# A fused conditioning block and graph attention on one core: modulation weights in two transfers, a new order and engine assignment, and V of two chunks spread by SBUF transfers

## What is computed

```python
# layer 0: block with adaptive modulation, 16 heads of 8
cmod = silu(c) @ w_ada + b_ada          # 6 x 128: shift, scale, gate, twice
x_mod = ln(x) * (1 + scale) + shift
k, q, v = split(x_mod @ w_qkv, 3)
y = softmax((q / 8) @ k.T) @ v
x = x + gate * (y @ w_proj + b_proj)
x = x + gate2 * (gelu(modulate(ln(x)) @ w_mlp1 + b_mlp1) @ w_mlp2 + b_mlp2)
# layer 1: graph attention, two directions, keys and values are the first 20 tokens
self = concat(x, where(rowsum(x) == 0, 0, c)) @ W_self.T + b_self
for d in range(2):
    aff = where(adj_d.sum(-1) > 0, q_d @ k_d.T / sqrt(8), NEG) + adj_d @ w_bias + b_bias
    out += per_head(softmax(aff) @ self[:, :20], Wout[d]) + bout[d]
return x + relu(self + out)
```

## Time and profile before

| | us |
|---|---|
| median of 3 runs | 98.25 |
| the three runs | 97.46, 98.25, 98.9 |
| the profiled execution | 97.81 |
| its span, first to last instruction | 96.1 |
| PE busy | 84.2 (88%) |
| DVE busy | 64.9 (68%) |
| POOL busy | 59.9 (62%) |
| ACT busy | 46.6 (49%) |

### The profile page before, as it was taken

The page is one execution under the profiler, slowest core; times in us unless marked ns, Lnnn a source line. Parts: engine busy times, 40 slices in busy tenths (PEclk is TensorE's granted clock), DMA queues, the critical chain, the costliest instruction groups (busy, mean ns, idle before and its releaser), DMA issues.

```text
span 96.1 us, 4165 instructions
## 1 busy us (share of the span) xinstructions
PE 84.2 (88%) x1806; PEld 67.8 (71%) x1806; DVE 64.9 (68%) x165; ACT 46.6 (49%) x103; POOL 59.9 (62%) x83
## 2 busy tenths in 40 slices
PE   0999974899999999799999999999999999959600
PEld 0999952577758867658887888787887878738600
DVE  2407989844995989847487500796869989757471
ACT  4600239569755339491804695353426545146300
POOL 6862996509980303547336199758099899876660
PEclk9999999669999999999999999999999999999975
DMA  1999995000000000000000011002000020322021
GB/s 39 268 303 391 335 283 147 0 0 3 7 7 0 7 0 10 0 0 7 3 0 0 10 24 43 7 0 59 20 12 0 21 50 14 84 59 61 3 61 55
DMA packets 3634, 5.75 MB, mean 60 GB/s; under 512 B 704, under 2 KB 2752, under 8 KB 3488
## 3 DMA queue, kind: packets, MB, share of 16 engines
q1 hardware_dynamic: 3352, 5.05, 18.4%
q10 hardware_dynamic: 264, 0.44, 1.3%
HBM read 4.22 MB, written 0.52 MB: 49 GB/s over the span
## 4 chain that ended last, share of the span: by engine, by line
PE 65%; DMA 10%; DVE 7%; POOL 5%; ACT 3%; SPq 3%; issue 3%; POOLq 1%
PE ps_s L965 12%; DMA home_a<-in_adj 10%; PE ps_b L887 7%; PE ps_b L893 7%; PE ps_b L867 6%; PE ps_b L820 5%; PE ps_b L983 4%; PE ps_b L912 4%; PE ps_b L837 3%; PE ps_b L1013 3%; PE ps_b L991 3%; PE ps_b L914 2%; PE ps_b L920 2%; ACT home_b L1115 2%; POOL home_a L625 2%
## 5 line engine op out<-in xcount | busy, mean ns | idle before, releaser
L619 POOL TENSOR_TENSOR E<-E,neg_max 128x640 f32<-128x640 f32 x8 | 10.2, 1276 | 5.7 <-DVE neg_max L1337 5.7
L1047 ACT ACTIVATE Kb<-ps_b,head_mask 128x256 f32<-128x256 f32 (+1 forms) x20 | 7.3, 434 | 7.5 <-PE ps_b L867 7.5
L1125 ACT ACTIVATE PT<-ps_b 120x384 f32<-120x384 f32 x16 | 7.4, 490 | 6.9 <-PE ps_b L983 6.8
L789 POOL TENSOR_TENSOR rstd<-var_eps,minus_half 128x2 f32<-128x2 f32 (+1 forms) x9 | 5.9, 667 | 6.7 <-DVE var_eps L1159 6.6
L723 POOL TENSOR_TENSOR Kb<-k_raw,head_mask 128x640 f32<-128x640 f32 x8 | 9.9, 1260 | 0.2 <-ACT k_raw L1078 0.2
L611 POOL TENSOR_TENSOR xT<-gated,xT 128x256 f32<-128x256 f32 x8 | 5.8, 727 | 6.3 <-DVE gated L1200 6.3
L723 POOL TENSOR_TENSOR Vz<-v_raw,quad_mask 128x1152 f32<-128x1152 f32 (+1 forms) x4 | 7.5, 1866 | 3.2 <-DVE v_raw L1192 3.2
L601 POOL TENSOR_TENSOR xm<-xm,cmod 128x256 f32<-128x256 f32 (+1 forms) x8 | 5.2, 648 | 6.0 <-DVE xm L1181 6.0
L887 PE MATMUL ps_b<-xm,w_rest_sb 128*128 128x256 f32 x32 | 8.7, 390 | 0.2
L1200 DVE SCALAR_TENSOR_TENSOR gated<-ps_b,cols,cmod 128x256 f32<-128x256 f32 x8 | 3.9, 481 | 7.1 <-PE ps_b L893 6.4
L1063 ACT ACTIVATE hidden<-ps_b,cols 128x256 f32<-128x256 f32 x16 | 7.1, 473 | 2.7 <-PE ps_b L887 2.5
(11 more groups left out here) (103 smaller groups left out, 201.1 us busy)
## 6 DMA issues: line engine op xcount, KB each, us to landing
w_rest_sb<-in_w_rest SPq DMA_DIRECT2D x1, 1088.0 KB, 7.3
home_a<-in_adj SPq DMA_DIRECT2D x2, 448.0 KB, 10.7
Vz<-v_raw SPq DMA_DIRECT2D x16, 33.8 KB
xT<-in_xT SPq DMA_DIRECT2D x1, 512.0 KB, 8.5
home_a<-in_adj SPq DMA_DIRECT2D x1, 512.0 KB, 11.0
w_ada_sb<-in_w_ada ACTq DMA_DIRECT2D x1, 384.0 KB, 3.1
out<-x_tok SPq DMA_DIRECT2D x3, 128.0 KB, 2.1
x_tok<-in_x_tok SPq DMA_DIRECT2D x1, 256.0 KB, 5.1
```

What stands on the lines that cost most here:

```text
L619: return engine.tensor_tensor(e, e, nm.unsqueeze(3).broadcast_to([P, u, H, M]), ALU.add)
L1047: return act.activation(Kb0[:, part, bs, :], ps_bs, ACT.Copy, scale=head_mask[:, 1, part:part + 1])
L1125: ins = act.activation(PT[0:KR, key % 3, 0:CH, :], ps[0:KR, 0:CH * P].rearrange("p (j t) -> p j t", t=P), ACT.Exp)
```

## The change

- `w_ada` arrives in two transfers: columns 0 to 255 on ACT's queue, as `ada0`, the rest on SP's queue behind the tokens, as `ada1`. `cmod` part 0 comes first on PE, part 1 behind the first q, k and v.
- ACT's first step is the zeroing of half of `Vz0` (`zero vz0`, 128 x 2304 elements); `silu` comes behind it, and `zero vz1a` moves from POOL to ACT.
- `WARM` goes from 9 to 5; the three `fill` steps (1, 8 and 3 products) go, and `FILL` puts 7, 1 and 2 products ahead of `v` 0, `cmod` 1 and `xnT` 2.
- `adjf` comes behind the eviction of `q` 4, in place of in the middle of the first chunks' evictions.
- `K_MASKED` shrinks to chunks 0 and 1: K of chunks 2 to 4 has one eviction on ACT and one masked product on POOL. V of chunks 0 and 1 is masked on ACT in four activations each, V of chunk 2 stays on POOL, V of chunks 3 and 4 is spread by four DMAs each from SP's queue.
- `qz` moves behind the first units. `sub` 6, 9 and 12, some of `ya`, `yb`, `resid1`, `shift` and evictions move to DVE, the evictions of `x1tok` to ACT, the first seven `relu` to ACT with the addition of `x` (`addx`) on POOL, `brep` to POOL.
- `ORDER` and `BANKS` are new throughout. Cut here to the beginning and the end of `ORDER`; `EVICTED` is empty, so `evict` isn't used.

```diff
-K_MASKED = {0, 1, 2, 3, 4}
+K_MASKED = {0, 1}
...
-ZERO_V = (0, 0)
-WARM = 9
-ON = {'adjf': 'act',
+ZERO_V = (4, 8)
+WARM = 5
+FILL = {('v', 0): 7, ('cmod', 1): 1, ('xnT', 2): 2}
+EVICTED = set()
...
+ ('brep', 0): 'pool',
+ ('relu', 0): 'act',
+ ('relu', 1): 'act',
+ ('relu', 2): 'act',
+ ('relu', 3): 'act',
+ ('relu', 4): 'act',
+ ('relu', 5): 'act',
+ ('relu', 6): 'act',
+ ('resid1', 0): 'dve',
+ ('resid1', 2): 'dve',
+ ('resid1', 3): 'dve',
  ('shift', (0, 0)): 'dve',
- ('spread', ('k1', 0, 0)): 'pool',
+ ('shift', (1, 1)): 'dve',
+ ('spread', ('k', 2)): 'pool',
+ ('spread', ('k', 3)): 'pool',
+ ('spread', ('k', 4)): 'pool',
+ ('spread', ('k1', 0, 0)): 'act',
  ('spread', ('k1', 0, 1)): 'pool',
- ('spread', ('k1', 1, 0)): 'pool',
+ ('spread', ('k1', 1, 0)): 'dve',
  ('spread', ('k1', 1, 1)): 'pool',
  ('spread', ('k1', 2, 0)): 'pool',
  ('spread', ('k1', 2, 1)): 'pool',
  ('spread', ('k1', 3, 0)): 'pool',
  ('spread', ('k1', 3, 1)): 'pool',
- ('spread', ('v', 0)): 'dve',
- ('spread', ('v', 1)): 'pool',
+ ('spread', ('v', 0)): 'act',
+ ('spread', ('v', 1)): 'act',
  ('spread', ('v', 2)): 'pool',
- ('spread', ('v', 3)): 'pool',
- ('spread', ('v', 4)): 'pool',
+ ('spread', ('v', 3)): 'sp',
+ ('spread', ('v', 4)): 'sp',
  ('spread', ('v1', 3, 1)): 'act',
  ('sub', 5): 'pool',
- ('sub', 6): 'pool',
+ ('sub', 6): 'dve',
  ('sub', 7): 'pool',
  ('sub', 8): 'pool',
- ('sub', 9): 'pool',
+ ('sub', 9): 'dve',
  ('sub', 10): 'pool',
  ('sub', 11): 'pool',
- ('sub', 12): 'pool'}
+ ('sub', 12): 'dve',
+ ('ya', 0): 'dve',
+ ('ya', 5): 'dve',
+ ('ya', 6): 'dve',
+ ('ya', 7): 'dve',
+ ('yb', 0): 'dve',
+ ('yb', 5): 'dve',
+ ('yb', 7): 'dve',
+ ('zero', 'vz0'): 'act',
+ ('zero', 'vz1a'): 'act'}
...
+ 'x1tok': 'act',
  'x2tok': 'act',
- 'yT': 'act'}
-BANKS = {('cmod', 1): 0,
- ('cmod', 0): 1,
- ('xnT', 0): 0,
- ('xnT', 1): 0,
+ 'yT': 'act',
+ (('k1', 1, 1), 0): 'dve',
+ (('k1', 2, 0), 0): 'dve',
+ (('k1', 2, 1), 0): 'dve',
+ (('q', 0), 0): 'dve',
+ (('q', 3), 0): 'dve',
+ (('q1', 0, 1), 0): 'dve',
+ (('q1', 1, 0), 0): 'dve',
+ (('q1', 1, 1), 0): 'dve',
+ (('x2tok', 0), 0): 'dve',
+ (('x2tok', 1), 0): 'dve',
+ (('x2tok', 2), 0): 'dve',
+ (('yT', 0), 0): 'dve',
+ (('yT', 2), 0): 'dve',
+ (('yT', 3), 0): 'dve'}
...
-ORDER = [('zero', 'v1_ones'), ('ident', 0), ('zero', 'pad'), ('zero', 'v0_ones'), ('masks', 0), ('consts', 0),
- ('zero', 'vz1b'), ('gbias', 0), ('plus1', 0), ('stats', (0, 0)), ('silu', 0), ('dense', ('cmod', 1)),
- ('rstd', (0, 0)), ('dense', ('cmod', 0)), ('sel', 0), ('take', (('cmod', 1), 0)), ('fill', (0, 1)), ('apply', 0),
- ('stats', (0, 1)), ('dense', ('xnT', 0)), ('fill', (1, 8)), ('take', (('cmod', 0), 0)), ('rstd', (0, 1)),
- ('stats', (0, 2)), ('zero', 'vz1a'), ('fetch', 0), ('take', (('xnT', 0), 0)), ('apply', 1), ('fetch', 2),
- ('shift', (0, 0)), ('dense', ('xnT', 1)), ('stats', (0, 3)), ('fetch', 1), ('dense', ('v', 0)),
- ('dense', ('k', 0)), ('dense', ('q', 0)), ('take', (('k', 0), 2)), ('fill', (2, 3)), ('take', (('v', 0), 0)),
- ('take', (('q', 0), 0)), ('take', (('xnT', 1), 0)), ('take', (('k', 0), 0)), ('spread', ('v', 0)),
- ('take', (('k', 0), 1)), ('dense', 'qz'), ('take', (('k', 0), 3)), ('stats', (0, 4)), ('take', ('qz', 0)),
- ('scores', 0), ('shift', (0, 1)), ('adjf', 0), ('rstd', (0, 2)), ('dense', ('k', 1)), ('max', 0),
- ('dense', ('q', 1)), ('dense', ('v', 1)), ('rstd', (0, 3)), ('take', (('k', 1), 1)), ('apply', 2),
- ('take', (('k', 1), 0)), ('take', (('v', 1), 0)), ('take', (('k', 1), 2)), ('rstd', (0, 4)), ('dense', ('xnT', 2)),
- ('sub', 0), ('adjf', 2), ('spread', ('v', 1)), ('apply', 3), ('turn', 0), ('take', (('xnT', 2), 0)),
- ('take', (('k', 1), 3)), ('apply', 4), ('take', (('q', 1), 0)), ('dense', ('xnT', 3)), ('shift', (0, 2)),
- ('scores', 1), ('take', (('xnT', 3), 0)), ('dense', ('q', 2)), ('max', 1), ('shift', (0, 3)), ('exp', 0),
- ('dense', ('k', 2)), ('sub', 1), ('dense', ('v', 3)), ('take', (('q', 2), 0)), ('take', (('k', 2), 3)),
- ('dense', ('v', 2)), ('take', (('v', 3), 0)), ('take', (('k', 2), 2)), ('turn', 1), ('take', (('v', 2), 0)),
- ('take', (('k', 2), 0)), ('spread', ('v', 3)), ('dense', ('k', 3)), ('take', (('k', 2), 1)), ('dense', ('xnT', 4)),
- ('exp', 1), ('scores', 2), ('take', (('xnT', 4), 0)), ('scores', 3), ('take', (('k', 3), 0)), ('values', 0),
- ('take', (('k', 3), 2)), ('max', 2), ('shift', (0, 4)), ('dense', ('q', 3)), ('take', (('k', 3), 1)),
- ('spread', ('v', 2)), ('take', (('k', 3), 3)), ('dense', ('k', 4)), ('take', (('q', 3), 0)), ('sub', 2),
- ('dense', ('v', 4)), ('adjf', 1), ('dense', ('q', 4)), ('values', 1), ('take', (('k', 4), 3)),
...
+ORDER = [('zero', 'vz0'), ('zero', 'v1_ones'), ('zero', 'v0_ones'), ('zero', 'pad'), ('ident', 0), ('consts', 0),
+ ('masks', 0), ('gbias', 0), ('sel', 0), ('plus1', 0), ('stats', (0, 0)), ('silu', 0), ('rstd', (0, 0)),
+ ('dense', ('cmod', 0)), ('zero', 'vz1b'), ('apply', 0), ('dense', ('xnT', 0)), ('take', (('cmod', 0), 0)),
+ ('take', (('xnT', 0), 0)), ('zero', 'vz1a'), ('stats', (0, 2)), ('shift', (0, 0)), ('stats', (0, 1)),
+ ('dense', ('v', 0)), ('dense', ('k', 0)), ('dense', ('q', 0)), ('take', (('v', 0), 0)), ('stats', (0, 3)),
+ ('fetch', 0), ('rstd', (0, 1)), ('dense', ('cmod', 1)), ('fetch', 2), ('rstd', (0, 2)), ('apply', 1), ('fetch', 1),
+ ('take', (('k', 0), 0)), ('take', (('q', 0), 0)), ('dense', ('xnT', 1)), ('take', (('cmod', 1), 0)),
+ ('take', (('k', 0), 3)), ('rstd', (0, 3)), ('apply', 2), ('take', (('k', 0), 2)), ('take', (('k', 0), 1)),
+ ('take', (('xnT', 1), 0)), ('dense', ('xnT', 2)), ('apply', 3), ('spread', ('v', 0)), ('shift', (0, 1)),
+ ('scores', 0), ('take', (('xnT', 2), 0)), ('dense', ('q', 1)), ('stats', (0, 4)), ('shift', (0, 2)),
+ ('dense', ('k', 1)), ('take', (('q', 1), 0)), ('dense', ('xnT', 3)), ('take', (('k', 1), 3)), ('dense', ('v', 1)),
+ ('dense', ('k', 2)), ('take', (('xnT', 3), 0)), ('take', (('k', 1), 1)), ('rstd', (0, 4)), ('take', (('k', 1), 2)),
+ ('max', 0), ('dense', ('v', 2)), ('take', (('k', 1), 0)), ('shift', (0, 3)), ('take', (('k', 2), 0)),
+ ('take', (('v', 1), 0)), ('dense', ('q', 2)), ('sub', 0), ('spread', ('v', 1)), ('spread', ('k', 2)),
+ ('dense', ('k', 3)), ('take', (('v', 2), 0)), ('scores', 1), ('apply', 4), ('turn', 0), ('take', (('k', 3), 0)),
+ ('max', 1), ('take', (('q', 2), 0)), ('dense', ('xnT', 4)), ('dense', ('v', 3)), ('spread', ('k', 3)), ('sub', 1),
+ ('dense', ('q', 3)), ('take', (('xnT', 4), 0)), ('scores', 2), ('take', (('q', 3), 0)), ('scores', 3), ('exp', 0),
+ ('take', (('v', 3), 0)), ('turn', 1), ('max', 2), ('spread', ('v', 3)), ('shift', (0, 4)), ('dense', 'qz'),
+ ('values', 0), ('exp', 1), ('spread', ('v', 2)), ('dense', ('q', 4)), ('take', ('qz', 0)), ('sub', 2),
+ ('values', 1), ('take', (('q', 4), 0)), ('dense', ('k', 4)), ('adjf', 0), ('recip', 0), ('scores', 4), ('mult', 0),
+ ('scores', 5), ('adjf', 2), ('dense', ('yT', 0)), ('max', 3), ('turn', 2), ('take', (('k', 4), 0)),
+ ('dense', ('v', 4)), ('exp', 2), ('spread', ('k', 4)), ('turn', 3), ('take', (('yT', 0), 0)), ('adjf', 1),
+ ('take', (('v', 4), 0)), ('dense', ('proj', 0)), ('sub', 3), ('spread', ('v', 4)), ('values', 2), ('exp', 3),
+ ('dense', ('bias', 0)), ('take', (('proj', 0), 0)), ('recip', 1), ('resid1', 0), ('turn', 4), ('mult', 1),
+ ('dense', ('x1tok', 0)), ('exp', 4), ('turn', 5), ('stats', (1, 0)), ('scores', 7), ('exp', 5), ('scores', 6),
...
+ ('dense', ('x2tok', 0)), ('turn', 19), ('badd', 11), ('ya', 3), ('turn', 18), ('dense', ('sbtok', 1)),
+ ('take', (('x2tok', 0), 0)), ('scores', 23), ('selfb', 2), ('max', 11), ('scores', 22), ('exp', 18),
+ ('values', 16), ('addx', 1), ('take', (('sbtok', 1), 0)), ('badd', 12), ('dense', ('sbtok', 2)), ('sub', 11),
+ ('exp', 19), ('dense', ('x2tok', 3)), ('take', (('sbtok', 2), 0)), ('values', 17), ('max', 12),
+ ('take', (('x2tok', 3), 0)), ('values', 18), ('yb', 3), ('turn', 20), ('recip', 9), ('selfb', 3), ('turn', 21),
+ ('relu', 3), ('sub', 12), ('exp', 20), ('addx', 3), ('values', 19), ('exp', 21), ('values', 20), ('mult', 9),
+ ('addx', 0), ('recip', 10), ('turn', 22), ('ya', 4), ('store', (0, 2)), ('mult', 10), ('turn', 23), ('yb', 2),
+ ('exp', 22), ('values', 21), ('ya', 5), ('yb', 4), ('exp', 23), ('yb', 5), ('values', 22), ('recip', 11),
+ ('relu', 2), ('dense', ('sbtok', 3)), ('relu', 5), ('addx', 2), ('mult', 11), ('relu', 4), ('values', 23),
+ ('take', (('sbtok', 3), 0)), ('addx', 5), ('ya', 6), ('store', (2, 4)), ('recip', 12), ('yb', 6), ('mult', 12),
+ ('addx', 4), ('relu', 6), ('ya', 7), ('addx', 6), ('store', (4, 6)), ('yb', 7), ('relu', 7), ('store', (6, 7)),
...
+        def by_transfer(key):
+            return key[0] == "v1" or engine_of("spread", key) == "sp"
...
+            if name == "act":
+                for i in range(HI):
+                    ins = engine.activation(to[:, i, :], of, ACT.Copy, scale=mask[:, i:i + 1])
+                return ins
...
+            sp.dma_start(w_ada_sb[:, 2 * P:6 * P], w_ada[:, 2 * P:6 * P]).then_inc(ld["ada1"], 16)
...
```

(25 more changed lines are left out.)

402 lines of the change are left out of this document (213 added, 189 removed), and 10 rows, old and new, of the table ORDER.

## The result

The change is **slower**: median 102.56 us (4 runs, 101.49 to 103.21) against 98.58 (4 runs, 97.46 to 98.99), ratio 1.041 with a 95% interval of 1.024 to 1.057. The forecast was 95.5 with 98.9 as its upper end. The profiled execution is the longest of the four, 103.21 us with a span of 101.5, against 97.81 and 96.1. Single executions of a kernel can fall into a slower state (the kernel before spreads from 95.9 to 101.2 us over this study), so the ratios compare fast executions alone, while the medians are of all executions of one measurement.

What follows compares the result with a forecast made beforehand. PE's own work bounds the kernel from 21 to 85 us, so gains come before and after: 2.1 (start) + 0 (middle) + 0.6 (end) = 2.7 off 98.25, giving 95.5 us; range 93.2 to 98.9.

Steps and rivals of the forecast that it cites:

- the sum of DVE's list: First V eviction to `sub` 2: 13.25 us of DVE steps plus 0.35 of waits, `sub` 2 at 24.0, 2.1 earlier.
- K and V of layer 0: Nine masks leave ACT, POOL's K products run 17.1 to 20.9, V 3 lands by some 25; nothing on the path.
- The start: Silu near 6.3 behind zeroing and two table loads; `v` 0 at 9.9, between 9.1 and 10.6, 0.9 earlier.
- Rival 3: Start: silu stands behind 2.3 us of zeroing and a load, `v` 0 at 10.6 or later; 97.2 us; chance 0.05.
- Rival 4: Start: about 1.38 us of drain behind each table load, silu ending near 7.7; 96.9 us; chance 0.05.
- The clock: After the first q, PE works 2.7 of 3.75 us, so the clock stays high; part of the 2.1 us.
- Rival 5: The start's hole, 4.7 to 6.4, keeps PE at 1.2 GHz, costing 0.48 per us; 100.5 if until 20; chance 0.10.
- The middle and the late half: From 26 to 85 us DVE gets near 8 us of steps and gives up some 5; effect taken as zero.
- Rival 2: Middle: added DVE and POOL steps make PE wait, 2 of the 8 us seen by PE; 97.5 us; chance 0.22.
- The end: Behind the last `mult`, three DVE steps take 0.9 instead of 1.41, 0.5 won; `sub` 12 on DVE adds 0.1.
- Adjacency and V transfers: Adjacency no longer holds up K 1, 1.5 us; V 3 lands by some 25 us, before `values` 4 needs it.

Runs made afterwards that it cites:

- the base: The changed kernel with `apply` 4 moved behind `max` 0 and POOL's K 2 product made to wait for it: 98.92 us, ratio 1.003 against the kernel before.
- the best: The base with silu ahead of the zeroing on ACT and `sub` 6, 9 and 12 on POOL again: 97.65 us, ratio 1.011 against the kernel before.
- the run at 98.19: The profiled one of six runs of the changed kernel with only the zeroing moved behind silu: 98.19 us, median 101.2.

## Why the prediction was wrong

**The step that failed** is the sum of DVE's list: "Placing each step of the list by these durations leaves 0.35 of waits", with `sub` 2 at 24.0. It starts from DVE's busy time of before, adds the new steps at their lengths alone, and never asks what POOL does beside them. The step beside it, "K and V of layer 0", put POOL's products at 17.1 to 20.9 and asked only who waits for them, not who runs beside them. POOL ran them at 18.28 to 22.07, and `apply 4`, 0.96 in the trace that the list was made from, took 3.23. The forecast read the length of `apply` in one place of that trace (0.34 for a step); in two others it was stretched, to 1.14 and 0.96 for two steps, and that was missed.

The collision costs 3.6 us of time between the change and the base. `sub` 2 gains 2.31 without it, and `scores` 4 3.05 (2.1 of hole, the rest work lost at 0.50 of the clock). The last scores gain 4.3, because in the base `sub` 9 gets in ahead of POOL's second mask (80.49) and not behind it (83.76), which saves PE's wait of 0.99; that this is chance of position is read from the rows and not tried.

Without the collision the list comes out nearly right, but by luck: from the first V eviction to `sub` 2 the base takes 13.50 us, forecast 13.60. DVE is busy 12.14 of them, forecast 13.25, and waits 1.36, forecast 0.35. The two misses cancel.

**The start** was mis-sized: `v` 0 at 11.23, forecast 9.9 as the middle of 9.1 and 10.6. It was the row of the lower clock, and the fillings began at 8.09, counted from 7.3. The order on ACT (zeroing, two loads, silu near 6.3) was right. Rival 3 had its mechanism: with silu first, `v` 0 comes 1.75 us earlier on the base and `scores` 4 2.2. Rival 4, a drain behind each table load, isn't in the rows: the load before silu ends at 5.96 and silu starts at 5.97.

**The clock.** "I take it that the clock stays high" was wrong twice. The passes were at half pace up to 13.19, in place of 7.21 before, and in the change the granted clock fell again at 23.43, behind a hole that no rival had. Rival 5 ("The hole from 4.7 to 6.4 keeps PE at 1.2 GHz") had this mechanism for the start. By its own price of 0.48 for each us, the 3.7 us from 9.5 to 13.2 make 1.8, an estimate. It isn't what made the kernel slower than before, since the base has the same start. Two readings of the forecast are wrong here: the pair of passes at 8.03, taken for the lower clock, stands behind 7.21 and is 0.47 long as a lone pair; and the passes of before turn fast at 7.21, not between 8.03 and 8.62.

**The middle and the late half.** "I take zero" was wrong by 2.1 us: in the base, first to last scores of layer 1 take 25.7 against 23.6. PE is idle 0.65 more, and does 1.5 more of its work there, which before was done ahead of the first scores of layer 1; that the order put it there is read from windows and not tried. Rival 2 (2 us seen by PE) had this size, but only 0.65 of it is PE waiting.

**The end.** The last `mult` to the last `relu` takes 1.15 us against 1.41: 0.3 won, forecast 0.5, and lost again in a tail of equal length.

**Adjacency and V transfers** had the right sign. The adjacency's place is worth 3.2 us where the start is early, counted as 1.5. The V transfers are not on the path; that V would have cost 2 us without them was not seen.

The 3.7 us between the range's upper end and the result are then the collision (3.6). That the base stands just at the upper end, 98.9, is chance: it misses the forecast of 95.5 by 3.4, of which some 1.4 are there at `sub` 2 (25.41, forecast 24.0) and 2.1 come in the middle.

## What to carry to other kernels

When work moves to GpSimd, list what VectorE runs beside it: each float32 step of it with two SBUF inputs, and each SBUF copy, may wait for the whole of a GpSimd product, and everything queued behind it waits too. The mark of it in a trace is one form of step with different lengths (`apply` here: 0.34 in one place, 1.14 for two in another). One wait on GpSimd that orders a long product behind a short VectorE step can be worth as much as a rearrangement was hoped to win (2.5 us here, forecast 2.7). Make such a step read PSUM on one side, or put it where GpSimd has short work.

## What the runs showed of the hardware

- The collision is all or nothing for a step with two SBUF inputs: 0.34 us alone, 2.32 beside a 2.34 us product. With one input in PSUM the step takes 0.28 in both.
- A windows row that prints 1.00 in the first microseconds says nothing of the clock: the trace has no record there. The 14 filling passes behind the same work on PE took 1.83, 3.10 and 3.35 us in three executions (silu first in the change, the best, silu first on the base). The first clock record stands at 5.82, 9.03 and 10.30 in them, and in each the distance between passes is 0.213 us before that record and 0.112 behind it. This moves `v` 0 by 1.5 us.

```profile
6.33 1.83 PE L1315 MATMUL ps_b<-ones 128*128 128x128 f32 x14 [0.45 <-DVE xm L1679]
```
```profile
6.33 3.35 PE L1318 MATMUL ps_b<-ones 128*128 128x128 f32 x14 [0.44 <-DVE xm L1682]
```

- Where the clock rises differs between executions of one start: 10.95 to 13.58 in the nine with the start of the change, 5.82 to 11.84 in the six with silu first. In the run at 98.19 it was earliest, which gives a part of its lead of at least 2.8 us over the other five; those have no profile, so the rest isn't shown.
- In every version with the changed order but the one without fillings, PE stands 0.6 to 1.4 us ahead of the third chunk of `bias` 1 (39.01 in the change) with no releaser, although its adjacency was converted long before. In all of them the hole ends 1.2 to 1.5 us behind the end of a 16 KB instruction transfer (queue 8: 37.57 in the change, 34.35 in the base, where the hole ends at 35.75), and so does the nameless wait at 70.5 without fillings (69.27). That PE waits for its program there is likely; no run tried it.
